# Linear attention on one core: two of four output banks scaled into SBUF, output products issued as two groups around a turning of keys

## The chip, the core and the metric

One NeuronCore of a Trainium2 chip runs the whole program. The metric is the device time of one execution in microseconds; less is better. The core has TensorE (PE; its weight loads are listed as PEld), VectorE (DVE), ScalarE (ACT), GpSimd (POOL) and SyncE (SP), each with its own instruction queue that is worked in order, and 16 DMA engines. SBUF is the working memory, PSUM the memory of eight banks into which TensorE writes.

## What is computed

The input is x, 8 batches of 1024 rows of 256 channels, all in float32. A convolution block is followed by four layers of linear attention, a feed-forward block with GELU, and a second feed-forward block whose weights are composed from 32 of 64 low-rank pieces. The change lies in the attention layers:

```python
def linear_attention(x, Wq, bq, Wk, bk, Wv, bv, g, bb):
    q = gelu(x @ Wq + bq) + 0.21
    k = gelu(x @ Wk + bk) + 0.21
    v = x @ Wv + bv
    q_r, k_r = rope(q), rope(k)
    # 16 heads of 16 channels
    kmean = jnp.mean(k, axis=2, keepdims=True)
    z = 1.0 / (jnp.einsum('bhnd,bhmd->bhnm', q, kmean) + 1e-06)
    kv = jnp.einsum('bhnd,bhne->bhde', k_r, v) / n
    out = jnp.einsum('bhnd,bhde->bhne', q_r, kv) * z
    return layernorm(out + x, g, bb)
```

## The kernel before

The program has three stages. The convolution stage fills the first 150 us or so, the attention stage runs to about 955 us, and then the pieces of the second feed-forward block are composed and the two feed-forward blocks run to the end.

The attention stage works in 32 **units**. A unit n is one layer of one batch (1024 rows); four batches are interleaved, so a unit depends on the unit four places before it. Each engine has a fixed order of work for a unit, written out by hand, and the engines meet through counting semaphores. `Waits.wait_ge` leaves out a wait that an earlier one already covers.

PSUM is held as four banks `big0` to `big3` and a ring of four banks `ring0` to `ring3`. In unit n the `big` banks hold, one after the other, the turned rows (`turn_u`), the outputs of unit n-1 (`outputs`) and the values of unit n (`values`). The ring serves in turn the four projections of keys, the four turnings of keys (`turn_k`), the four projections of queries, the denominators and the key-value sums.

**PE in unit n** (from line 935): `key_value(n-1)`, `turn_u(n, 1)`, four projections of keys of six 512-column products each, `turn_k` 0 and 1, `outputs(n-1)`, `turn_k` 2 and 3, four projections of queries, `values` 0 to 3 of twelve 256-column products each, `turn_u(n+1, 0)`, `denominators(n)`. `outputs` is 32 products on 32x32 corners of the array, each recorded twice, so 64 records (L928); the first half of them belongs to the first block of channels, the second half to the second. `values(n, u)` writes over `big[u]`, so it waits until bank u of unit n-1 has been added to the residual (`s_y`).

**DVE in unit n** (from line 1150): the end of the normalisation of older units, then `rotate_k` 0 (L1076, L1077), `k_mean`, `rotate_k` 1, and the steps of `FINISH` for unit n-1. For each bank i these are `turn` (L1096, a 32x32 block transpose in the bank), `scale` (L1103, times z) and `add_h` (L1109, the bank plus the residual row block `y_of`, which is in SBUF). `rotate_k` 2 and 3 stand between the first of them. Then come `rotate_q` (L1090, L1091, the rotation of the second half of the queries into `qc` and `qs`) and `split_u(n+1, 0)` (L1065). `turn` waits for `s_out`, which the last output product raises.

**POOL in unit n**: `residual` (L789, L792), four `sum_k` (L773), `rotate_q` of the first half of the queries (L799, L800), `sum_q(n)` (L807), `invert`. `sum_q` waits for DVE's `rotate_q` and issues two DMAs that add `qs` into `qc`. `outputs(n)`, one unit later, waits for their landing (`d_qr`). Six times in the stage, POOL also issues the load of a layer's weights (L760), right after `invert`. The operands of L773, L799 and L800 are all in SBUF.

**The end of the stage.** PE runs `key_value(31)`, then `outputs(31)`, and then enters the composing stage through `then(e, lambda: None)`: `compose_phase` calls the function given to it (`last`) after its first `multiply`. That first `multiply` is twelve 512-column products (L32, L33, L34 into `acc`), and it waits for DVE's first two splittings (L1832, L1834).

## Time and profile before

| what | value |
|---|---|
| median of 3 runs | 1804.67 us |
| lowest and highest | 1802.76 and 1806.49 us |
| the profiled execution's own time | 1804.48 us |
| its span, first to last instruction | 1802.5 us |
| mean granted TensorE clock | 0.994 |
| busy PE, PEld, DVE | 1772.3, 1440.9, 1483.2 us |
| busy ACT, POOL | 922.5, 997.3 us |

The span is 2 us less than the time of the same execution. The busy times are sums over stages that differ: POOL is busy 9 tenths and more in the slices from about 160 to 850 us and mostly idle after, DVE is around 9 tenths in the attention stage and PE shows almost no idle time anywhere. A product's recorded duration is longer than its place in the stream, since products overlap in the array: what one costs is the distance from its start to the next start. Times of rows are microseconds from the span's start, durations are microseconds in timelines and nanoseconds in groups.

### The profile page before, as it was taken

How to read it: one execution, taken by the hardware profiler on the slowest of the kernel's cores; microseconds unless marked ns; L12 is line 12 of the kernel's file. 1: busy time of each engine (PE TensorE's matmuls, PEld its weight loads, DVE VectorE, ACT ScalarE, POOL GpSimd, SP SyncE). 2: the span in 40 equal slices, each digit the busy share in tenths (PEclk: the TensorE clock that was granted, in tenths of full speed). 3: DMA queues.
4: the chain of work that ended last, by engine and by line, in shares of the span. 5: the costliest groups of instructions: out<-in, count | busy, mean ns of one | idle time of the engine just before them, and what ended most of it. 6: DMA issues, size and time to landing. Idle time of an engine off the chain costs nothing.

```text
span 1802.5 us, 42043 instructions
## 1 busy us (share of the span) xinstructions
PE 1772.3 (98%) x17084; PEld 1440.9 (80%) x17084; DVE 1483.2 (82%) x3486; ACT 922.5 (51%) x1741; POOL 997.3 (55%) x775
## 2 busy tenths in 40 slices
PE   9999999999999999999998999999999999999998
PEld 3336788888888888888886988888888888888887
DVE  3667799999999999999997749696979788888887
ACT  4555666777766777766776723332333333332231
POOL 1556999999999999999991022121313121212221
PEclk9999999999999999999999999999999999999999
DMA  7363442122325422323238711010101010101000
GB/s 285 148 255 146 135 113 48 39 70 48 84 49 153 137 65 49 83 49 76 70 92 274 241 62 48 24 47 24 47 24 47 24 48 24 36 35 36 30 7 24
DMA packets 30193, 148.59 MB, mean 82 GB/s; under 512 B 5488, under 2 KB 6320, under 8 KB 20784
## 3 DMA queue, kind: packets, MB, share of 16 engines
q1 hardware_dynamic: 20960, 89.62, 14.1%
q0 software_dynamic: 6272, 46.14, 11.5%
q10 hardware_dynamic: 2768, 10.15, 1.5%
q8 instruction: 134, 2.20, 0.5%
q14 instruction: 59, 0.48, 0.1%
HBM read 80.89 MB, written 31.46 MB: 62 GB/s over the span
## 4 chain that ended last, share of the span: by engine, by line
PE 92%; DVE 3%; DMA 2%; POOL 1%; issue 1%; ACT 1%; ACTq 0%; SPq 0%; DVEq 0%; POOLq 0%
PE bankC L1433 13%; PE bankC L33 7%; PE bankC L32 7%; PE bankC L34 7%; PE ring L32 6%; PE ring L34 6%; PE ring L33 6%; PE bankC L1432 6%; PE big L32 3%; PE big L853 3%; PE big L33 3%; PE big L34 3%; PE ring L873 3%; PE hid_ps L245 3%; PE conv_ps L256 3%; PE big L928 2%
## 5 line engine op out<-in xcount | busy, mean ns | idle before, releaser
L1433 PE MATMUL bankC<-down,act_hi 128*128 128x512 f32 x992 | 353.1, 397 | 0.0
L1432 PE MATMUL bankC<-down,act_lo 128*128 128x256 f32 x868 | 246.2, 284 | 0.0
L1433 PEld LDWEIGHTS bankC<-down,act_hi 128*128 128x128 f32 x992 | 186.3, 188 | 41.9
L1558 DVE TENSOR_TENSOR act_lo<-gel,act_hi 128x512 fp32r<-128x512 f32 x256 | 210.6, 823 | 8.7
L33 PE MATMUL bankC<-aT_lo,up_hi 128*128 128x512 f32 x512 | 199.6, 390 | 0.0
L32 PE MATMUL bankC<-aT_hi,up_hi 128*128 128x512 f32 x512 | 199.5, 390 | 0.0
L34 PE MATMUL bankC<-aT_hi,up_lo 128*128 128x512 f32 x512 | 199.4, 389 | 0.0
L1512 POOL TENSOR_TENSOR hC<-hC,vecC 128x1024 f32<-128x1024 f32 x16 | 38.7, 2416 | 283.9 <-PE turn L1407 283.9
L1518 POOL TENSOR_TENSOR rstdC<-var_epsC,minus_halfC 128x4 f32<-128x4 f32 x47 | 56.1, 1194 | 249.2 <-DVE var_epsC L1586 249.2
L1432 PEld LDWEIGHTS bankC<-down,act_lo 128*128 128x128 f32 x868 | 164.1, 189 | 1.4
L773 POOL TENSOR_TENSOR kr<-kr,kc 128x512 f32<-128x512 f32 x128 | 161.8, 1296 | 0.2 <-DVE kr L1077 0.2
L1475 ACT ACTIVATE aT_hi<-turn 128x512 fp32r<-128x512 f32 x64 | 34.8, 596 | 234.8 <-PE turn L1407 234.8
L1483 ACT ACTIVATE gel<-bankC,b1s 128x512 f32<-128x512 f32 x128 | 88.5, 691 | 128.7 <-PE bankC L34 112.6
L792 POOL TENSOR_TENSOR yB<-yB,shift 128x1024 f32<-128x1024 f32 x64 | 152.2, 2408 | 0.0
L1483 ACT ACTIVATE gel<-bankC 128x512 f32<-128x512 f32 x128 | 76.8, 600 | 141.7 <-PE bankC L34 125.0
L1004 ACT ACTIVATE yB<-yB,offset,rstdB 128x256 f32<-128x256 f32 x256 | 129.5, 590 | 0.0
L973 ACT ACTIVATE gkT<-ring,bias_qk 128x512 f32<-128x512 f32 x128 | 88.2, 690 | 79.7 <-PE ring L34 79.7
L1547 DVE TENSOR_TENSOR aT_lo<-turn,aT_hi 128x512 fp32r<-128x512 f32 x64 | 41.1, 683 | 105.2 <-ACT aT_hi L1475 105.2
L1076 DVE SCALAR_TENSOR_TENSOR kc<-ring,cos_k 128x512 f32<-128x512 f32 x128 | 86.6, 677 | 42.7 <-PE ring L873 42.7
L998 ACT ACTIVATE v<-big 128x512 f32<-128x512 f32 x128 | 76.5, 598 | 85.6 <-PE big L34 85.5
L789 POOL TENSOR_TENSOR yB<-yB,gain 128x1024 f32<-128x1024 f32 x48 | 114.5, 2405 | 0.1
L34 PEld LDWEIGHTS bankC<-aT_hi,up_lo 128*128 128x128 f32 x512 | 96.1, 188 | 20.2
(211 smaller groups left out, 5224.0 us busy)
## 6 DMA issues: line engine op xcount, KB each, us to landing
qc<-qs POOLq DMA_DIRECT2D x64, 512.0 KB, 6.5
raw_late<-in_AB SPq DMA_DIRECT2D x30, 320.0 KB, 3.8
u<-hA SPq DMA_DIRECT2D x8, 1024.0 KB, 4.8
u_next<-u SPq DMA_DIRECT2D x8, 1024.0 KB, 5.7
hC<-u SPq DMA_DIRECT2D x16, 512.0 KB, 4.2
xC<-in_x SPq DMA_DIRECT2D x16, 512.0 KB, 5.1
out<-w_flat SPq DMA_DIRECT2D x15, 512.0 KB, 2.6
w_flat<-in_AB SPq DMA_DIRECT2D x22, 320.0 KB, 4.2
```

Source lines behind the costliest of these rows:

```text
L32: e.matmul(out, wh, xh, start=start, stop=False)
L33: e.matmul(out, wh, xl, start=False, stop=False)
L34: return e.matmul(out, wl, xh, start=False, stop=stop)
L773: e.tensor_tensor(kr[:, u, :], kr[:, u, :], kc[:, u, :], ALU.add).then_inc(s_kr, 1)
L789: e.tensor_tensor(tiles(y, a), tiles(src, a), row(gain), ALU.mult).then_inc(s_mul, 1)
L792: e.tensor_tensor(tiles(y, a), tiles(y, a), row(shift), ALU.add).then_inc(s_res, 1)
L973: e.activation(gkT[:, db, half(x)], ring_of(n, "k", 2 * x + db)[:, :], ACT.Gelu, bias=bias_qk[:, at:at + 1], accum_out=k_sums[:, db, x:x + ...
L1004: e.activation(y[:, o, :], y[:, o, :], ACT.Identity, bias=offset[:, two, o:o + 1], scale=rstd[:, two, o:o + 1]).then_inc(s_unit, 1)
L1432: e.matmul(bank[:, 0:H], a_lo[:, fb, tok], both[k][:, fb, 0, :], start=False, stop=False)
L1433: m = e.matmul(bank[:, :], a_hi[:, fb, tok], both[k][:, fb, :, :].rearrange("p a h -> p (a h)"), start=fb == 0, stop=fb == FB - 1)
L1483: e.activation(gel[:, n % GEL, :], bank_of(i, k, s, fb)[:, :], ACT.Gelu if k == 0 else ACT.Gelu_apprx_tanh, bias=b1s[:, fb:fb + 1] if k == ...
L1558: e.tensor_tensor(a_lo[:, fb, :], g, a_hi[:, fb, :].bitcast(F32), ALU.subtract).then_inc(s_act_lo, 1)
```

## The change

Six edits, all in the attention stage:

1. `scale` of banks 2 and 3 writes its result into SBUF, into the second half of `qs` (`apart`), in place of the bank itself; `add_h` of banks 2 and 3 reads it there.
2. `values` 2 and 3 wait for the scaling of their bank (`s_scaled`), no more for the adding.
3. DVE's `rotate_q` gets a wait for those two adds (the same engine, earlier in its order), since it writes where they read.
4. The order of `FINISH`: `turn` 2 before `add_h` 0, and `scale` 3 before `add_h` 2. `rotate_k` 3 now comes before `turn` 1.
5. `outputs(n-1)` is issued as two groups of 16 products, with `turn_k(n, 2)` between them. The semaphore for DVE is raised by the last product of the second group.
6. `outputs(31)` is handed to the composing stage, which runs it after its first `multiply`.

```diff
@@ -690,6 +690,9 @@
+        HELD = 2
+        apart = lambda i: qs[:, i - HELD, half(1)]
@@ -876,7 +879,10 @@
             def values(n, u):
                 wt = weights(n, 2 * H, H)
-                w.wait_ge(s_y, 4 * (n - 1) + u + 1)
+                if u < HELD:
+                    w.wait_ge(s_y, 4 * (n - 1) + u + 1)
+                else:
+                    w.wait_ge(s_scaled, 4 * (n - 1) + u + 1)
                 w.wait_ge(s_lo, 4 * n + 4)
@@ -912,7 +918,7 @@
-            def outputs(n):
+            def outputs(n, blocks=range(CB)):
...
-                for db in range(CB):
+                for db in blocks:
                     for j in range(QUARTERS):
...
-                m.then_inc(s_out, 1)
+                if CB - 1 in blocks:
+                    m.then_inc(s_out, 1)
@@ -940,8 +947,10 @@
                 turn_k(n, 1)
                 if n >= 1:
-                    outputs(n - 1)
+                    outputs(n - 1, [0])
                 turn_k(n, 2)
+                if n >= 1:
+                    outputs(n - 1, [1])
                 turn_k(n, 3)
@@ -952,8 +961,7 @@
             key_value(UNITS - 1)
-            outputs(UNITS - 1)
-            then(e, lambda: None)
+            then(e, lambda: outputs(UNITS - 1))
@@ -1086,6 +1094,7 @@
                 w.wait_ge(s_out, n)
+                w.wait_ge(s_y, 4 * (n - 1) + HELD + db + 1)
                 w.wait_ge(d_q, 2 * 16)
@@ -1098,15 +1107,17 @@
+                to = out if i < HELD else apart(i).rearrange("p (a n d) -> p a n d", a=TILES, d=HD)
...
-                e.tensor_tensor(out, out, zb, ALU.mult).then_inc(s_scaled, 1)
+                e.tensor_tensor(to, out, zb, ALU.mult).then_inc(s_scaled, 1)
 
             def add_h(n, i):
                 heads = y_of(n)[:, :, 64 * i:64 * i + 64]
+                sums = big[i][:, :] if i < HELD else apart(i)
...
-                e.tensor_tensor(heads, big[i][:, :].rearrange("p (a m) -> p a m", a=TILES), heads, ALU.add).then_inc(s_y, 1)
+                e.tensor_tensor(heads, sums.rearrange("p (a m) -> p a m", a=TILES), heads, ALU.add).then_inc(s_y, 1)
@@ -1146,8 +1157,8 @@
-            FINISH = [[(turn, 0)], [(turn, 1), (scale, 0)], [(add_h, 0), (turn, 2)], [(scale, 1), (add_h, 1)],
-                      [(turn, 3), (scale, 2)], [(add_h, 2), (scale, 3)], [(add_h, 3)]]
+            FINISH = [[(turn, 0)], [(turn, 1), (scale, 0)], [(turn, 2), (add_h, 0)], [(scale, 1), (add_h, 1)],
+                      [(turn, 3), (scale, 2)], [(scale, 3), (add_h, 2)], [(add_h, 3)]]
@@ -1170,10 +1181,10 @@
                     rotate_k(n, u)
-                    if n >= 1 and u < 3:
-                        finish(n - 1, u - 1)
+                    if n >= 1 and u == 1:
+                        finish(n - 1, 0)
                 if n >= 1:
-                    for k in range(2, 7):
+                    for k in range(1, 7):
                         finish(n - 1, k)
```

## Rows read from the trace of the kernel before

**Rows 1.** Timeline of DVE, unit 19: start, duration, engine, line, operands [idle before].

```profile
637.01 0.72 DVE L1096 STREAM_TRANSPOSE big<-big 128x512 f32<-128x512 f32 x1
...
644.37 0.67 DVE L1103 TENSOR_TENSOR big<-big,z 128x512 f32<-128x512 f32 x1
645.07 0.69 DVE L1109 TENSOR_TENSOR yB<-big,yB 128x512 f32<-128x512 f32 x1
...
646.41 0.69 DVE L1109 TENSOR_TENSOR yB<-big,yB 128x512 f32<-128x512 f32 x1
647.01 0.68 DVE L1090 SCALAR_TENSOR_TENSOR qc<-ring,cos_q 128x512 f32<-128x512 f32 x1
```

**Rows 2.** Waits by engine, line and releaser, 192 to 1010 us: total, times, longest.

```profile
PEld ring L32 <- DVE kr L1077: 7.7, 29, 0.3
...
PEld big L32 <- DVE yB L1109: 1.8, 12, 0.2
```

**Rows 3.** Timeline of POOL, units 18 to 20.

```profile
625.55 1.78 POOL L807 DMA_DIRECT2D qc<-qs  x2 [1.36 <-DVE qs L1091]
...
643.70 1.30 POOL L799 TENSOR_TENSOR qc<-gT,cos_q 128x512 f32<-128x512 f32 x1
...
650.04 1.78 POOL L807 DMA_DIRECT2D qc<-qs  x2 [1.28 <-DVE qs L1091]
...
668.92 1.29 POOL L799 TENSOR_TENSOR qc<-gT,cos_q 128x512 f32<-128x512 f32 x1
```

**Rows 4.** Line L807, the two DMAs issued at 650.0 and 650.7.

```profile
DMA to landing us min/median/max: 5.2/6.6/7.9
```

**Rows 5.** Timeline of PE, unit 19; the third row is from a cut at 635.25.

```profile
633.90 1.04 PE L873 MATMUL ring<-identity,gkT 128*128 128x128 f32 x8
634.87 1.49 PE L928 MATMUL big<-qc,kv 32*32 32x256 f32 x64
...
634.87 0.71 PE L928 MATMUL big<-qc,kv 32*32 32x256 f32 x32
...
636.30 1.09 PE L873 MATMUL ring<-identity,gkT 128*128 128x128 f32 x8
```

**Rows 6.** Timelines of PE and DVE where outputs waited for their DMA.

```profile
857.73 1.49 PE L928 MATMUL big<-qc,kv 32*32 32x256 f32 x64 [1.71 <-DMA qc<-qs]
...
859.27 0.73 DVE L1096 STREAM_TRANSPOSE big<-big 128x512 f32<-128x512 f32 x1 [1.09 <-PE big L928]
```

**Rows 7.** Line L1558: nanoseconds min/median/max; then one of its long ones, beside POOL's.

```profile
L1558 DVE TENSOR_TENSOR act_lo<-gel,act_hi x256: 691/693/2782, 1061.1 to 1785.0; 128x512 fp32r<-128x512 f32 x128
...
1090.03 2.77 DVE L1558 TENSOR_TENSOR act_lo<-gel,act_hi 128x512 fp32r<-128x512 f32 x1
...
1089.74 2.52 POOL L1523 TENSOR_TENSOR w_flat<-w_flat,xC 128x1024 f32<-128x1024 f32 x1 [4.16 <-DVE w_flat L1598]
```

**Rows 8.** Timelines of DVE and POOL at 158 us.

```profile
158.67 1.76 DVE L600 TENSOR_TENSOR bias_v<-bv_in,head_block 128x256 f32<-128x256 f32 x1
...
157.76 4.92 POOL L789 TENSOR_TENSOR yB<-u_next,gain 128x1024 f32<-128x1024 f32 x2 [1.46 <-PE big L853]
```

**Rows 9.** Timelines of DVE and POOL at 1049 us.

```profile
1049.10 1.35 DVE L1832 SCALAR_TENSOR_TENSOR duo_lo<-w_flat,w_col,duo_hi 128x1024 fp32r<-128x1024 f32 x1 [5.82 <-ACT duo_hi L1801]
1050.38 2.56 DVE L1834 TENSOR_TENSOR duo_lo<-w_flat,duo_hi 128x256 fp32r<-128x256 f32 x1
...
1049.45 3.20 POOL L1514 TENSOR_TENSOR hC<-hC,vecC 128x1024 f32<-128x1024 f32 x1
```

**Rows 10.** Timelines of DVE and PE at the end of the attention stage.

```profile
949.61 1.22 DVE L1834 TENSOR_TENSOR duo_lo<-u_next,duo_hi 128x1024 fp32r<-128x1024 f32 x1
...
954.04 2.38 PE L928 MATMUL big<-qc,kv 32*32 32x256 f32 x64 [5.53 <-DMA qc<-qs]
956.35 0.79 PE L32 MATMUL acc<-duo_hi 128*128 128x512 f32 x1
...
959.82 0.39 PE L32 MATMUL acc<-duo_hi 128*128 128x512 f32 x1
```

## The prediction

> **What bounds the kernel now.** I read the page first (each engine's share and its slices), then a timeline of one attention unit on PE, on DVE and on POOL, then the list of waits, and last the rows in which DVE and POOL touch. The attention units are the part to cost, since all edits but one repeat there. One unit lasts 24.49 us: POOL's DMA issue comes at 625.55 and again at 650.04 [rows 3]. PE is the bound: its only repeated waits over the stage are 0.27 us for a rotated key (29 times) and 0.15 us for an added bank (12 times listed) [rows 2]. DVE and POOL have little room behind it. POOL is idle once a unit, 1.28 us ahead of the DMA issue, because DVE's rotation of queries is not done [rows 3]. And the DMA has less room still: the second of the two is issued at 650.65 and lands 7.9 us after [rows 4], at 658.55, while the outputs that need it start one period after 634.87 [rows 5], at 659.36. So four things run in one ring with small gaps: POOL, DVE, the DMA and PE.
>
> **What the change removes.** The two waits of PE. The third rotation of keys moves ahead of two finishing steps, and values 2 need no add. The two waits are at most 0.27 + 0.15, about 0.4 us a unit [rows 2]; part of it overlaps with products in flight, so I take 0.3. PE alone could then do a unit in about 24.2 us.
>
> **What the split of the outputs adds.** The 64 records start within 1.12 us (1.49 less one duration of 0.37), the first 32 within 0.34 (0.71 less 0.37), and turning starts at 636.30, which is 0.31 after the last start [rows 5]. A group of 32 alone thus takes 0.34 + 0.31 = 0.65, two take 1.30, where the 64 take 1.43: the second half of the 64 is slower than the first, as if the queue ran dry, and the turning between would let it fill. Against that stands one more change between full products and corners: the eight turnings ahead need 0.97 (633.90 to 634.87), at 0.11 each they would need 0.88 [rows 5], so 0.1, and some 0.05 on the way back. Sum: +0.02 us a unit. If the second group runs at the pace of the slow half, it is +0.34; with no cost of changing, -0.13. I take +0.02, because the slow half begins only after 32 records. The rule of the Trainium skill (TensorEngine Tiling (Array Packing), Key Properties) that changing the tiling mode drains the engine speaks against this edit; the trace has its 0.31 us, already in the sum above, and no run here separates the two.
>
> **What moves on DVE.** Turning of the keys comes between the groups, so the semaphore for DVE comes later: 0.65 + four turnings (0.59 with both changes) + 0.34 + 0.37 + 0.05 = 2.0 us after the outputs begin, where it was 1.54 (857.73 to 859.27) [rows 6]. From 634.87 that is 636.87, still ahead of 637.01, when DVE gets there [rows 1]. This delay is hidden as long as the outputs don't start late. The new wait of `rotate_q` for the adds costs nothing: they stand ahead of it in DVE's own queue. Behind each of DVE's adds, though, everything of DVE is queued, and POOL's DMA issue waits for the rotation.
>
> **What the change adds, and what I hold to decide it.** The adds of banks 2 and 3 read two operands from SBUF; before, one was in PSUM. POOL at that time runs products whose operands are both in SBUF, without a gap. The trace shows what two such operations do to each other. L1558 takes 0.69 us, but 2.77 at 1090.03, when POOL's 2.52 us add had begun at 1089.74; it ends 0.54 after POOL's, so it really ran from 0.15 before POOL's end. At 158.67 DVE waits inside the first of two adjoining operations of POOL and ends at 160.43, long before the second ends at 162.68: it gets in between the two [rows 8]. At 1049.45 POOL waits until DVE's first is done, and DVE's second, behind it in the queue, waits until POOL's is done at 1052.65 [rows 9]. They exclude each other and take turns [rows 7 to 9]. The Trainium skill says so too (SBUF — State Buffer, "SBUF: two separate sides": the pair of ports is an exclusive lock against DVE operations with two SBUF inputs), not who goes next; by that rule as by the rows, the sum is the one below, and without the exclusion it is the first rival.
>
> **The ring, step by step.** Count from POOL's DMA issue D.
> - POOL's first product of queries starts at D + 18.15 (625.55 to 643.70) and takes 1.30 [rows 3]. DVE can get in at D + 18.15 + 1.30 - 0.15 = D + 19.30.
> - DVE asks for its first SBUF add 8.57 us after the first turn: 8.06 as before (637.01 to 645.07), plus 0.6 for the scaling that now precedes it, less 0.1, since add 2 no longer stands right behind its own scaling (0.70 against 0.60 us) [rows 1].
> - Add 2 runs at D + 19.30. POOL then takes its turn: held until add 2 is nearly done, 0.69 - 0.2, then 1.30, less 0.15. Add 3 starts about 1.66 after add 2.
> - The rotation starts 0.60 after that, and the next D is 3.03 later (647.01 to 650.04) [rows 1, 3].
>
> Sum: 19.30 + 1.66 + 0.60 + 3.03 = 24.59 us a unit, against 24.49. So PE's gain of 0.3 isn't had: PE is early, and waits at the outputs. The DMA's way round agrees: it lands at D + 8.5 (7.9 plus 0.61 between the issues), outputs, 2.0 to the first turn, 8.57 to the request, D + 19.13 with 0.05 for the wake-up, only 0.17 ahead of D + 19.30.
>
> **The sum.** 29 units at +0.10: +2.9. Six units have the weight load on POOL, where the first product comes at 18.88 (650.04 to 668.92) [rows 3]; in a ring without room its 0.73 counts: +4.4. The first two units, in which the ring has to settle: two delays of POOL of 0.4 each, twice, an estimate: +1.5. The unit in which the DMA waits anyway (1.71 us) [rows 6] loses about 1 more, since the DMA is issued later; small hiccups of PE elsewhere, an estimate of the same size, are now covered by its waits: together 0. Sum of the units: +8.8.
>
> The end of the stage: the DMA lands at 954.04, the outputs and the first twelve composing products are done at 959.82, 5.8 us later [rows 10]. After the change the twelve run while the DMA is under way: their operand is ready at 949.61 + 1.22 = 950.83, they need 2.7 at full rate (0.227 each). Behind the landing stay the outputs, 1.5 to 2.3. That saves 3.5 to 4.3; the first products behind an idle PE are slow (0.79 for the first at 956.35 against 0.39), which may push them past the landing, and I take 3.2, from 1.5 to 4.3. Nothing behind it changes: the composing stage is PE's.
>
> Total: +8.8 - 3.2 = +5.6 on the profiled execution, 1804.48 + 5.6 = 1810.1; that execution lies 0.2 under the median of the runs, so 1810.
>
> **The rivals.**
> - *The exclusion is small or DVE gets both adds at once.* Then the ring needs at most 19.30 + 0.6 + 0.6 + 3.03 = 23.5, PE is the bound at 24.2, 29 units save 8 us and the end 4: 1793 (1790 to 1800). Against it: [rows 7, 9]. For it: no row shows two adjoining DVE adds beside short POOL products. 0.25.
> - *The request comes too late.* If the outputs' split costs 0.17 more, or the DMA lands 0.17 later, DVE asks after D + 19.30 and waits for the next product, 1.25 more a unit. In all units that is +36: 1846; in half of them about 1828. This is where the split decides, though its own time is nothing. 0.2.
> - *POOL's queue always wins.* DVE then waits for the end of all four products (18.15 + 5.0) and a unit is about 27.4: +85, 1890. [rows 8] speak against it. 0.05.
> - *No change*, since the gains and exclusions meet: 1805. 0.05.
>
> The forecast itself, 1803 to 1816, has 0.45.
>
> **How the numbers follow.** A measurement tells about 0.2%, 3.6 us. The forecast's own range lies two thirds above +3.6. Slower: 0.32 of the forecast, 0.2 and 0.05: 0.57. Same: 0.1 + 0.05 + 0.03 = 0.18. Faster: 0.03 + 0.22 = 0.25. The range leaves out the last tenth of the first rival and the worst of the late ones: 1792 to 1836.
>
> **What would show it.** L1109 in two groups, one near 0.69 and one over a microsecond long; POOL's L799 or L800 lengthened by about 0.4; a period of 24.6; a PE wait of 0.3 to 0.5 for the DMA ahead of L928 in most units. If L1109 stays at 0.69 throughout, the first rival holds. Periods near 25.8 are the second. If PE waits for neither the rotated key nor an added bank, the removed waits are right, whatever the time. At the end, L928 stands behind twelve products into acc.

## The result and the profile after

| what | before | after |
|---|---|---|
| median of 6 runs, us | 1804.85 | 1846.67 |
| lowest and highest, us | 1802.76, 1808.12 | 1840.18, 1852.39 |
| span of the profiled execution, us | 1802.5 | 1844.4 |
| mean granted TensorE clock | 0.994 | 0.988 |
| busy DVE, POOL, us | 1483.2, 997.3 | 1563.3, 1013.8 |

The ratio is 1.0227, with a 95% interval of 1.0203 to 1.0252: slower by 41 us. The forecast was 1810 with a range of 1792 to 1836. The direction was right, the time lies outside the range.

**The adds.** The line of the adds (L1109 of before is L1120 here), nanoseconds min/median/max, first the banks read in PSUM, then those read in SBUF:

```profile
L1120 DVE TENSOR_TENSOR yB<-big,yB x64: 659/680/693, 197.8 to 1021.2; 128x512 f32<-128x512 f32 x64
L1120 DVE TENSOR_TENSOR yB<-qs,yB x64: 669/1777/6000, 201.6 to 1029.2; 128x512 f32<-128x512 f32 x64
```

DVE is busy 80 us more than before, and the second row accounts for that and a little more: the page of the profile has it as 131.8 us for 64, mean 2097 ns, where 64 at the first row's 0.68 would be 44.

**A unit that went as forecast.** Timelines of DVE and POOL of the kernel after, unit 19; columns as in [rows 1, 3]. The DMA issue before it came at 647.35.

```profile
665.78 1.57 DVE L1120 TENSOR_TENSOR yB<-qs,yB 128x512 f32<-128x512 f32 x1
...
665.49 1.32 POOL L802 TENSOR_TENSOR qc<-gT,cos_q 128x512 f32<-128x512 f32 x1
666.74 1.77 POOL L803 TENSOR_TENSOR qs<-gT,sin_q 128x512 f32<-128x512 f32 x1
668.47 1.73 POOL L802 TENSOR_TENSOR qc<-gT,cos_q 128x512 f32<-128x512 f32 x1
...
672.01 1.77 POOL L810 DMA_DIRECT2D qc<-qs  x2 [0.56 <-DVE qs L1100]
```

Add 2 is asked for 0.29 into POOL's first product and ends at 667.35, so it really began at 666.66: 19.31 after the DMA issue, where the forecast had 19.30. POOL's second product carries the delay (1.77 for 1.28). The unit lasts 672.01 - 647.35 = 24.66; forecast 24.59.

**A unit that did not.** The same two timelines, unit 20:

```profile
690.46 5.99 DVE L1120 TENSOR_TENSOR yB<-qs,yB 128x512 f32<-128x512 f32 x1
...
690.88 1.29 POOL L802 TENSOR_TENSOR qc<-gT,cos_q 128x512 f32<-128x512 f32 x1
692.13 1.28 POOL L803 TENSOR_TENSOR qs<-gT,sin_q 128x512 f32<-128x512 f32 x1
693.38 1.26 POOL L802 TENSOR_TENSOR qc<-gT,cos_q 128x512 f32<-128x512 f32 x1
694.61 1.28 POOL L803 TENSOR_TENSOR qs<-gT,sin_q 128x512 f32<-128x512 f32 x1
700.00 1.75 POOL L810 DMA_DIRECT2D qc<-qs  x2 [4.11 <-DVE qs L1100]
```

DVE asks at 690.46, during POOL's last sum of keys, and is served only when POOL's last product is over: four operations of POOL begin and end meanwhile, none of them lengthened. Behind the add stands the rotation of queries, for which POOL then waits idle, 4.11 us. The unit lasts 27.99. I call such an add **passed over** (it lasts over 2.2 us). In the kernel after these are the adds of units 4, 6, 8, 12, 16, 20, 22, 24, 25, 30 and 31: eleven, among them all six in which POOL issues a weight load. The mark of 2.2 us misses the mildest case: unit 28 asks during POOL's third product, sees the fourth go first and lasts 2.10, so by what happens there are twelve.

**Where the 41 us are.** From the DMA issue of unit 2 to that of unit 31 before took 713.13 and after takes 757.95: +44.8. The 713.13 are 24.59 a unit on the average, the forecast's own period: the 24.49 of the forecast is an ordinary unit of the kernel before, and a few of its units last longer, up to 25.8. So the division counts over 24.59 (25.3 with a weight load). Eleven units passed over, at 28.0 or 27.3, cost 2.7 each: 29.5. Four units right behind such a one (7, 17, 21, 23) last 25.9, since DVE asks at the end of POOL's first product or later: 5.2. Unit 13, of the same kind, 27.1: 2.5. Unit 28, 27.2: 2.6. The six weight loads, at the forecast's 0.73 each (the served ones in e15 last 25.2): 4.4. The twelve other units, 24.57 to 24.69: 0.6. Sum 44.8. Before unit 2 the kernel gains 0.9, and from the DMA issue of unit 31 to the end it gains 2.1. 44.8 - 0.9 - 2.1 = 41.8, and the spans differ by 41.9.

**Why the next unit is late too.** Behind a passed-over add PE stands idle for 2.1 to 3.2 us ahead of its projections of keys. The table by windows has us, then busy time of PE, PEld, DVE, ACT and POOL with counts, then the granted TensorE clock, the DMA share and GB/s; first the window behind the add of unit 6, then that behind the add of unit 4:

```profile
338.16:341.16 3.00, 3.00 (x9) 2.31 (x9) 2.96 (x10) 0.78 (x2) 2.92 (x4) 0.54 1.00 199
286.25:289.25 3.00, 2.84 (x13) 2.02 (x13) 2.96 (x10) 1.47 (x4) 2.92 (x4) 1.00 0.97 194
```

Of ten such places, five have a granted clock of 0.50 to 0.65 there, most of the time its lower level of 1.2 GHz, and they are just the five ahead of units 7, 13, 17, 21 and 23. The keys' 512-column products then start 0.43 apart and not 0.23, the outputs begin 8.7 to 10.0 after the DMA issue and not 7.7, and DVE asks 0.9 to 2.2 later. In the other five the clock stays at 1.00 and the next unit isn't late. Why it fell in some and not in others the rows don't tell; the idle times before are alike. (Ahead of unit 21 the DMA lands 8.4 after its issue, where 7.0 to 7.9 is usual, and would have made that unit late by itself.) In unit 28 it is the DMA alone: it lands 10.1 after its issue, and PE waits 2.36 for it.

**What was removed is gone.** Waits by engine, line and releaser over the attention stage, 192 to 1030 us; neither row of [rows 2] has an answer here. What PE waits for now is of another kind:

```profile
PEld ring L32 <- issue: 41.2, 33, 3.4
...
PE ring L32 <- DVE hT_lo L1073: 30.2, 24, 3.2
```

PE stands ahead of the projections of keys, because DVE's splitting of the input stands behind the adds in DVE's queue. The forecast had PE wait at the outputs for the DMA in most units; in the same list that wait comes 11 times and to 5.6 us in all (PEld, L934).

**The outputs in two groups.** PE's timeline of unit 19, answering [rows 5], and DVE's first turn:

```profile
655.09 0.71 PE L934 MATMUL big<-qc,kv 32*32 32x256 f32 x32
655.73 0.66 PE L876 MATMUL ring<-identity,gkT 128*128 128x128 f32 x4
656.32 0.71 PE L934 MATMUL big<-qc,kv 32*32 32x256 f32 x32
...
656.96 0.44 PE L876 MATMUL ring<-identity,gkT 128*128 128x128 f32 x2
...
657.22 0.73 DVE L1105 STREAM_TRANSPOSE big<-big 128x512 f32<-128x512 f32 x1
```

0.64 + 0.59 + 0.64, as forecast (0.65, 0.59, 0.65). The first turn starts 2.13 after the outputs; forecast 2.0, before 1.54.

### The profile page after: what moved, and what is told of

The parts are those of the page before. It is cut to its first block, busy times and chain, and to the rows that moved or that the text cites. A ratio compares the mean times of both kernels' runs of the same rounds, so it can differ in the third digit from the quotient of the medians.

```text
span 1844.4 us, 42105 instructions
## 1 busy us (share of the span) xinstructions
PE 1783.0 (97%) x17084; PEld 1437.6 (78%) x17084; DVE 1563.3 (85%) x3486; ACT 922.7 (50%) x1741; POOL 1013.8 (55%) x775
## 4 chain that ended last, share of the span: by engine, by line
PE 69%; DVE 22%; issue 5%; DMA 3%; POOL 1%; ACT 1%; ACTq 0%; SPq 0%; DVEq 0%; POOLq 0%
PE bankC L1444 13%; PE bankC L32 7%; PE bankC L33 7%; PE bankC L34 7%; DVE yB L1120 6%; PE bankC L1443 6%; PE ring L32 4%; PE ring L33 3%; PE ring L34 3%; DVE kr L1085 3%; PE conv_ps L256 3%; PE hid_ps L245 3%; DVE big L1105 2%; DMA qc<-qs 2%; DVE hT_lo L1073 2%
## 5 line engine op out<-in xcount | busy, mean ns | idle before, releaser
L1444 PEld LDWEIGHTS bankC<-down,act_hi 128*128 128x128 f32 x992 | 186.3, 188 | 41.9
L795 POOL TENSOR_TENSOR yB<-yB,shift 128x1024 f32<-128x1024 f32 x64 | 152.6, 2416 | 0.0
L1120 DVE TENSOR_TENSOR yB<-qs,yB 128x512 f32<-128x512 f32 x64 | 131.8, 2097 | 0.0
L1558 DVE TENSOR_TENSOR aT_lo<-turn,aT_hi 128x512 fp32r<-128x512 f32 x64 | 41.1, 684 | 105.2 <-ACT aT_hi L1486 105.2
L32 PE MATMUL ring<-hT_hi,w_second 128*128 128x512 f32 x256 | 106.8, 417 | 17.7 <-DVE hT_lo L1073 17.4
L32 PE MATMUL ring<-hT_hi,w_first 128*128 128x512 f32 x256 | 104.5, 408 | 14.0 <-DVE hT_lo L1073 13.7
```

The lines of the kernel that those rows point to most:

```text
L32: e.matmul(out, wh, xh, start=start, stop=False)
L795: e.tensor_tensor(tiles(y, a), tiles(y, a), row(shift), ALU.add).then_inc(s_res, 1)
L1120: e.tensor_tensor(heads, sums.rearrange("p (a m) -> p a m", a=TILES), heads, ALU.add).then_inc(s_y, 1)
L1444: m = e.matmul(bank[:, :], a_hi[:, fb, tok], both[k][:, fb, :, :].rearrange("p a h -> p (a h)"), start=fb == 0, stop=fb == FB - 1)
```

## The experiments

No kernel leaves out part of the computation. Ratios are to the kernel before on the same chip, with 95% intervals; e13, e14 and e16 to e19 rest on two executions each, the others on four or more. Counts and periods are from one profiled execution of each kernel. "Units passed over" counts adds of bank 2 over 2.2 us in units 3 to 31: six with a weight load, 23 others. The diffs are against the kernel after, where nothing else is said.

### First question: is it the SBUF adds, the split, the order or the end?

**e1_psum_adds**: all four banks scaled in place and added from PSUM; order, split and end as in the kernel after.

```diff
-        HELD = 2
+        HELD = 4
...
-                w.wait_ge(s_y, 4 * (n - 1) + HELD + db + 1)
```

> The changed kernel with banks 2 and 3 scaled in place in PSUM again and added from there, values waiting for the adds; the new order of the finishing steps, the two groups of outputs and the moved last outputs stay. If the exclusion between DVE's adds with two SBUF operands and POOL's products makes the loss, the add takes 0.69 us in every unit, a unit takes 24.2 to 24.4 us and the time is 1793 (1789 to 1799). If the split of the outputs or the new order makes it, the time stays at 1835 to 1850.

Measured: 1815.14, ratio 1.0050 (1.0033 to 1.0067). No add lasts over 0.7. So 32 of the 41 us at the least belong to the two SBUF operands. But the unit lasts 24.95, not 24.2 to 24.4, so this kernel pays some 13 us that the kernel after doesn't, and the operands' share is larger (e3 gives 51). The waits of this kernel show why: values wait for an added bank once in nearly every unit, at most 0.7. The two rows are the weight load and the product behind it in the same wait.

```profile
PEld big L32 <- DVE yB L1119: 22.3, 30, 0.7
PE big L32 <- DVE yB L1119: 16.2, 30, 0.5
```

In the new order the add of bank 2 stands behind the scaling of bank 3, and a rotation of keys stands ahead of both. That order needs the early release of the bank which the scaling into SBUF gives; alone it costs 0.46 a unit. I had not expected it.

**e6_psum_one_group**: the same with the outputs in one group.

```diff
-                    outputs(n - 1, [0])
-                turn_k(n, 2)
-                if n >= 1:
-                    outputs(n - 1, [1])
+                    outputs(n - 1)
+                turn_k(n, 2)
```

> The kernel after with all four banks scaled in place and added from PSUM, and the outputs in one group: beside the first run (the same with two groups, 1815.1, period 24.95) it takes the split away. If the order of scaling and adding (values 2 waiting 0.7 us for their bank) is the whole of its +0.46 a unit, this one stays at 1813 to 1816. If the split with its later first turn is what makes the adds late, the wait of values 2 shrinks by up to 0.5 and the time falls to 1803 to 1806.

Measured: 1812.73, ratio 1.0040 (1.0027 to 1.0054), period 24.95 again. The order is the cost, not the split.

**e2_one_group**: the kernel after with that same edit.

> The changed kernel with the 32 output products in one group ahead of the third turning, everything else kept. If the exclusion alone makes the loss, the ring from one DMA issue to the next stays at 24.65 us in the units where DVE gets in after one product, units with an add of 5 to 6 us stay too, and the time is 1830 to 1855. If the split makes DVE ask too late for a place between two products, the time falls to 1815 or less and the adds of 5 us are gone.

Measured: 1842.91, ratio 1.0204 (1.0184 to 1.0224), an interval that overlaps that of the kernel after. Served units last 24.6, and eleven are passed over (4, 5, 8, 10, 12, 13, 16, 18, 20, 24, 26). The split is not the cause.

**e9_split_only**: the kernel before with the outputs in two groups and nothing else (the edit of e6, the other way round).

> The kernel before with the outputs in two groups around the third turning, nothing else. By the prediction's sum the PE stream grows by 0.02 us a unit (-0.13 to +0.34) and DVE's first turn comes 0.5 later after the start of the outputs, hidden if DVE arrives later anyway: 1805 to 1806. The rival, that the later turn reaches DVE, POOL's DMA issue and back to PE: up to +0.5 a unit, 1820. In the trace the period of a unit (24.49 before) tells: 24.50 by the first, up to 25.0 by the rival.

Measured: 1805.35, ratio 1.0004 (0.9995 to 1.0013), period 24.5. The split costs nothing that can be measured, and gains nothing.

**e5_end_only**: the kernel before with the end's edit.

```diff
-            outputs(UNITS - 1)
-            then(e, lambda: None)
+            then(e, lambda: outputs(UNITS - 1))
```

> The kernel before with the edit of the end alone (outputs of unit 31 behind the first twelve composing products). The sum of the prediction says -3.2 us (1.5 to 4.3), so 1801.3; the kernel after lost 2.05 between D(31) and the end, and if that is this edit's worth, 1802.4. The rival that the products behind the landing are no quicker in sum says 1804.5. In the trace: L928 of unit 31 behind twelve products into acc, end of L928 to end of span shorter by 2 to 3.

Measured: 1801.06, ratio 0.9982 (0.9973 to 0.9991), so -3.2 (-4.9 to -1.6). Its PE timeline, answering [rows 10]:

```profile
954.26 0.47 PE L34 MATMUL acc<-duo_hi,duo_lo 128*128 128x512 f32 x1
954.66 1.49 PE L928 MATMUL big<-qc,kv 32*32 32x256 f32 x64
956.09 0.50 PE L32 MATMUL acc<-duo_hi 128*128 128x512 f32 x1
```

Twelve products and the outputs are done at 956.1, before at 959.8. In the kernel after only 2.1 is gained between the DMA issue of unit 31 and the end. There PE had been idle for 6.67, and its first nine products ran at 1.2 GHz, as the table by windows shows. That isn't where the rest was lost, though: all twelve are over before the DMA lands, and the outputs wait for it.

```profile
993.00:997.00 4.00, 3.78 (x9) 3.05 (x10) 4.00 (x8) 0.00 (x0) 3.12 (x2) 0.50 0.92 175
...
993.22 0.77 PE L32 MATMUL acc<-duo_hi 128*128 128x512 f32 x1 [6.67 <-DVE duo_lo L1845]
...
998.79 1.49 PE L934 MATMUL big<-qc,kv 32*32 32x256 f32 x64 [0.74 <-DMA qc<-qs]
```

From the DMA issue of unit 31 to the thirteenth composing product it is 13.6 in the kernel before, 10.3 in e5 and 10.1 in the kernel after: up to there the edit gives 3.4 and 3.6. The kernel after loses 1.4 of it again somewhere behind; where, wasn't followed. In e7, where unit 31 is served, 2.4 is gained from that DMA issue to the end.

### Second question: can the adds be taken out of POOL's way?

**e3_adds_after_rotation**: banks 2 and 3 are held in another buffer (the second half of `gkT`, free until the next projections of keys), and both adds stand behind the rotation of queries. POOL's products are then over when DVE asks, or the last of them is running, and nothing of the ring waits for the adds. ScalarE, which writes the next keys there, waits for the adds.

```diff
-        apart = lambda i: qs[:, i - HELD, half(1)]
+        apart = lambda n, i: (gkT if n + 1 < UNITS else qs)[:, i - HELD, half(1)]
...
                 for db in range(CB):
                     rotate_q(n, db)
+                if n >= 1:
+                    finish(n - 1, 6)
```

> The changed kernel with the scaled banks 2 and 3 kept in the second half of gkT (idle by then) and both adds moved behind the rotation of queries, where POOL issues its DMAs and has no product with two SBUF operands. If the exclusion makes the loss, the adds take 0.69 us, POOL's DMA issue comes 1.2 us earlier in the ring, and the time is 1792 (1788 to 1798), under the kernel before. If an add from SBUF is slow for itself, or DMA issue excludes DVE as well, the adds stay over 1 us and the time is 1815 or more.

Measured: 1795.9, ratio 0.9951 (0.9932 to 0.9970). It beats both kernels. The DVE timeline of unit 19; POOL's next DMA issue is at 668.85:

```profile
665.79 0.68 DVE L1100 SCALAR_TENSOR_TENSOR qc<-ring,cos_q 128x512 f32<-128x512 f32 x1
...
668.18 1.52 DVE L1121 TENSOR_TENSOR yB<-gkT,yB 128x512 f32<-128x512 f32 x2
...
668.85 1.75 POOL L810 DMA_DIRECT2D qc<-qs  x2 [0.30 <-POOL qs L803]
```

The two adds take 1.52 together; in unit 19 of the kernel after they took 3.27. POOL now waits for its own last product and not for DVE; the period is 24.15, which agrees with the 24.2 I gave PE alone. Against the kernel after this is 51 us less with the same computation: the price of the adds standing where POOL's chain and the ring are.

**e10_after_rotation_one_group**: e3 with the outputs in one group.

> The version with its two SBUF adds behind the rotation of queries (1795.9, ratio 0.995, period 24.15), with the outputs in one group again. There PE bounds the unit, so the split shows by its own cost: the prediction's +0.02 a unit says 1795 to 1796 (ratio 0.995); if two groups are quicker as the groups alone were (0.65 twice for 1.43, so -0.13), this one is slower, up to 1800; if the later turn costs, it is quicker, 1790 or less.

Measured: 1797.38, ratio 0.9956 (0.9941 to 0.9972), period 24.15. With and without the split the times can't be told apart, where PE is the bound too.

### Third question: why is DVE passed over in some units and not in others?

**e4_breath**: a memset of one column (0.09 us) on POOL ahead of each of its four products. Extra work.

```diff
+                e.memset(breath[:, 2 * db:2 * db + 1], 0.0)
                 e.tensor_tensor(qc[:, db, cols], gT[:, db, cols], table_q(cos_q, db, x), ALU.mult)
+                e.memset(breath[:, 2 * db + 1:2 * db + 2], 0.0)
                 e.tensor_tensor(qs[:, db, cols], gT[:, db, cols], table_q(sin_q, db, x), ALU.mult).then_inc(s_qr, 1)
```

> The changed kernel with a one-column memset on POOL ahead of each of its four products of queries, so that no product follows directly on another. If DVE's add is passed over because POOL's next product is already in line, there is no add over 2.2 us left, all units take 24.7 to 25.9 us, and the time is 1810 to 1825. If being passed over has another cause, adds of 5 to 6 us stay in some 10 units and the time is 1840 or more.

Measured: 1838.4, ratio 1.0182 (1.0165 to 1.0199). Passed over: 0 of 23 ordinary units, but 6 of 6 with a weight load. Neither theory foretold that split. It says that there are two cases, and that the load units are one by themselves. (Unit 2, which the count leaves out, was passed over with the memsets in place, 3.6 us.)

**e7_again**: the kernel after once more.

> The kernel after once more, unchanged, to see which units are passed over in another execution. If a fixed property of the program decides, the same eleven (4, 6, 8, 12, 16, 20, 22, 24, 25, 30, 31) are passed over and the span is 1844 within 1. If the phase of the moment decides, the six with the load stay and the others change, by number too, with 3 us for each unit more or less: 1840 to 1852.

Measured: 1847.08, ratio 1.0224 (1.0206 to 1.0243). The six with the load are passed over again, and of the others 3, 13, 14, 17, 18 and 21, where the first execution had 6, 22, 25, 30 and 31. The load units are fixed, the rest is not.

**e11_load_later** and **e12_pool_later**: the load moves the products 0.7 later. Is it this place that loses, or the load?

```diff
-                if lane(n) == 0 and 2 <= n // LANES + 1 < B // LANES * L:
-                    load_w(n // LANES + 1)
...
                     rotate_q(n, 0, db)
+                if lane(n) == 0 and 2 <= n // LANES + 1 < B // LANES * L:
+                    load_w(n // LANES + 1)
                 sum_q(n)
```

> The kernel after with POOL's six weight loads behind the products of queries instead of ahead of the residual. In three kernels all six units with the load had their add of bank 2 passed over (5.8 to 6.1 us), 18 of 18, and in all of them it was asked for during the last sum of keys, since the load put POOL's products 0.7 later. Theory one, the place in POOL's chain decides: the six become like the others (mostly served after the first product, 24.65), which gives back about 6 x 3.4 = 20: 1826, 1818 to 1836, and at most two or three of the six are passed over. Theory two, the load itself or chance decides: the six stay near 28, 1840 to 1850.

Measured: 1853.69, ratio 1.0249 (1.0218 to 1.0281): no quicker than the kernel after, whose interval overlaps, and above both expectations. Passed over: 1 of 6 load units and 5 of 23 others, so the load's place matters. But the time was lost again at once: the queries' DMA now queues behind the weight load. Line L810 has

```profile
DMA to landing us min/median/max: 4.5/6.7/13.1
```

where the longest in the kernel after is 9.5. PE waits for it at the outputs in five units, here in unit 5:

```profile
294.51 1.17 PE L934 MATMUL big<-qc,kv 32*32 32x256 f32 x32 [5.33 <-DMA qc<-qs]
```

```diff
                     load_w(n // LANES + 1)
+                elif n >= 3:
+                    w.wait_ge(s_memset, 1)
+                    for s in range(2):
+                        e.tensor_tensor(spare[:, s:s + 1], tiny[:, :], minus_half[:, 0:1], ALU.pow)
                 residual(n)
```

> The kernel after with about 0.7 us of extra work on POOL (two powers of one column) at the head of every unit that has no weight load, so that in all units the add is asked for during the last sum of keys. Extra work, nothing left out. Theory one, the place decides: nearly all units from the fourth on are passed over, period about 28, time 1804.7 + 29 x 3.5 = about 1905 (1890 to 1915), which is the third rival of the prediction. Theory two, the place doesn't decide: the share of units passed over stays at a third and the others run at 25.3, time 1860 to 1875.

Measured: 1870.39, ratio 1.0351 (1.0334 to 1.0368). Passed over: 6 of 6 and 9 of 23. Of the ordinary units whose request fell into a sum of keys, eleven were served and three passed over. The place does not decide; theory one fell, and the load itself was left.

**e14_load_after_residual** puts the load behind the residual, right ahead of the sums of keys. **e13_small_load** puts a small DMA at the load's place in all other units from unit 3 on.

```diff
-                if lane(n) == 0 and 2 <= n // LANES + 1 < B // LANES * L:
-                    load_w(n // LANES + 1)
                 residual(n)
+                if lane(n) == 0 and 2 <= n // LANES + 1 < B // LANES * L:
+                    load_w(n // LANES + 1)
```

> The kernel after with the weight load issued between POOL's residual and its sums of keys, 10 us later than in the kernel after, so that its transfer (9 us) is in flight while the add is asked for. If the load as such decides wherever it stands ahead of the sums, all six units stay passed over (28.0): 1840 to 1852. If only its place ahead of the residual does, they become like the others: 1825 to 1840.

Measured: 1851.3, ratio 1.0257 (1.0227 to 1.0287); 6 of 6 and 8 of 23.

```diff
                     load_w(n // LANES + 1)
+                elif n >= 3:
+                    w.wait_ge(d_spare, 16 * small[0])
+                    small[0] += 1
+                    e.dma_start(spare[:, :], w_split[0:1, :, 0:2].rearrange("l p c -> (l p) c")).then_inc(d_spare, 16)
                 residual(n)
```

> The kernel after with a small DMA (two columns) issued by POOL at the head of every unit from the fourth on that has no weight load, at the load's place. Extra work, nothing left out. Seen so far: with the load ahead of the chain the add was passed over in 30 of 30 units (five kernels), with 0.7 us of arithmetic in its place (the run with POOL later) in about 9 of 23, and with the load behind the products in 1 of 6. If an issued DMA ahead of the residual is what keeps DVE out until the chain ends, nearly all units are passed over now: period about 28, 1895 to 1915. If it is the load's own bulk or chance, about a third as before: 1855 to 1880.

Measured: 1900.24, ratio 1.0528 (1.0490 to 1.0566). Passed over: 6 of 6 and 22 of 23, period 27.9 to 28.0 throughout (the one missing, unit 28, lasts 2.0 and was passed by one product). A DMA of two columns, issued by POOL 14.7 us ahead of DVE's request, is enough. From the timelines of POOL and DVE, unit 17:

```profile
628.57 0.63 POOL L830 DMA_DIRECT2D spare<-w_split  x1
...
643.27 5.93 DVE L1126 TENSOR_TENSOR yB<-qs,yB 128x512 f32<-128x512 f32 x1
```

**e15_load_before_invert** and **e16_invert_first**. The queries' two DMAs stand ahead of POOL's chain in every unit, though, and do no such harm. Between them and the chain lies `invert`: a power (L818), then a product that waits for that power (L820). e15 puts the load ahead of `invert`, e16 takes `invert` from between the queries' DMAs and the chain.

```diff
                 sum_q(n)
+                if lane(n + 1) == 0 and 2 <= (n + 1) // LANES + 1 < B // LANES * L:
+                    load_w((n + 1) // LANES + 1)
                 if n >= 2:
                     invert(n - 2)
```

> The kernel after with the weight load moved two POOL instructions earlier, behind the two DMAs of queries and ahead of the power (L818) and product of invert, so that it delays no DMA of queries. Small DMAs ahead of the residual made 28 of 28 adds be passed over, but the DMAs of queries, which stand ahead of the power, don't. Theory one: a DMA issued with no power behind it is what keeps DVE out; then the six units are served like the others (at most three passed over) and the time falls by about 18: 1820 to 1835. Theory two: any load DMA ahead of the chain does it: all six passed over, 1840 to 1855.

Measured: 1824.85, ratio 1.0107 (1.0077 to 1.0137). Passed over: 0 of 6 and 4 of 23. Two POOL instructions' difference in place gives back 22 us. Rows of POOL and DVE, unit 16, which has a load:

```profile
561.06 1.21 POOL L763 DMA_DIRECT2D w_second<-w_split  x1
561.65 2.31 POOL L818 TENSOR_TENSOR rstdB<-var_epsB,minus_halfB 128x8 f32<-128x8 f32 x1
564.04 0.20 POOL L820 TENSOR_TENSOR offset<-minus_mean,rstdB 128x8 f32<-128x8 f32 x1
...
578.71 1.75 DVE L1120 TENSOR_TENSOR yB<-qs,yB 128x512 f32<-128x512 f32 x1
```

```diff
-                sum_q(n)
                 if n >= 2:
                     invert(n - 2)
+                sum_q(n)
```

> The kernel after with POOL's invert ahead of its DMAs of queries, so that in every unit a DMA stands directly ahead of the residual and the chain. The chain then starts 2.5 us earlier after the DMA issue (15.7), the request falls into the third product, and being passed over costs little: add 2 ends at D + 20.5 and not 19.3. Theory one: nearly all units are passed over (add 2 takes about 2.7 us, only 0.68 for add 3), period 24.8, with the load 25.4: 1811 to 1820. Theory two: about a third are, and the others show add 2 at about 1.5 and add 3 at 1.78: 1806 to 1815. The count of long adds tells them apart, not the time.

Measured: 1831.63, ratio 1.0138 (1.0118 to 1.0159). Passed over: 6 of 6 and 21 of 23. The count is what theory one said; the time was 12 over its range, since the period is 25.3 (25.9 with the load) and not 24.8. POOL's and DVE's rows of unit 18:

```profile
634.49 1.83 POOL L802 TENSOR_TENSOR qc<-gT,cos_q 128x512 f32<-128x512 f32 x1
635.75 1.82 POOL L803 TENSOR_TENSOR qs<-gT,sin_q 128x512 f32<-128x512 f32 x1
637.00 2.62 POOL L818 TENSOR_TENSOR rstdB<-var_epsB,minus_halfB 128x8 f32<-128x8 f32 x1
...
634.80 3.32 DVE L1120 TENSOR_TENSOR yB<-qs,yB 128x512 f32<-128x512 f32 x1
```

The products start 1.26 apart and are recorded as lasting 1.83: here each overlaps the next by 0.57, where in the kernel after it is 0.03. The two units that weren't passed over say more. In units 28 and 29 POOL stood idle between the DMAs and the chain, 1.66 for DVE and 0.55 for PE. There the records overlap by 0.04 to 0.05 again, and the add of unit 29 got in (that of 28 asked during the last product). POOL's rows of unit 29:

```profile
900.10 4.76 POOL L792 TENSOR_TENSOR yB<-yB,gain 128x1024 f32<-128x1024 f32 x2 [0.55 <-PE big L856]
...
914.50 1.30 POOL L802 TENSOR_TENSOR qc<-gT,cos_q 128x512 f32<-128x512 f32 x1
```


**e17_small_load_power**, **e18_small_load_product** and **e19_small_load_own_wait** take e13 and put parts of `invert` behind the DMA. All have extra work.

```diff
+                if n >= 3:
+                    w.wait_ge(s_memset, 1)
+                    e.tensor_tensor(other[:, :], tiny[:, :], minus_half[:, 0:1], ALU.pow)
                 residual(n)
```

> The kernel with the small DMA in every unit (1900 us, 29 of 29 adds passed over from unit 3 on but 28), with a power of one column behind that DMA, also behind the weight load, and no wait of POOL for itself. Extra work, nothing left out. Theory one, a power behind the DMA undoes its effect: the count falls to a third or less (0 to 12 of 29), period of the others about 25.8: 1845 to 1875. Theory two, it was the wait of invert for its own result or its second instruction that did it: the count stays at 28 or 29, 1905 to 1920.

Measured: 1917.01, ratio 1.0623 (1.0590 to 1.0656); 6 of 6 and 23 of 23. With `mult` in place of `pow`:

> The same with an ordinary product of one column in the power's place. If any instruction of another size or kind behind the DMA undoes the effect, the count falls as with the power. If only the power does, the count stays at 28 or 29 of 29 and the time at 1900 to 1912; the residual behind the DMA is ordinary arithmetic too and doesn't undo it, so this is what I expect.

Measured: 1906.18, ratio 1.0563 (1.0530 to 1.0596); 6 of 6 and 22 of 23. Neither undoes the DMA's effect.

```diff
+                if n >= 3:
+                    w.wait_ge(s_memset, 1)
+                    e.tensor_tensor(other[:, 0:1], tiny[:, :], minus_half[:, 0:1], ALU.pow).then_inc(s_own, 1)
+                    own[0] += 1
+                    w.wait_ge(s_own, own[0])
+                    e.tensor_tensor(other[:, 1:2], other[:, 0:1], tiny[:, :], ALU.mult)
                 residual(n)
```

> The kernel with the small DMA and the one-column power (29 of 29 adds passed over), and behind them a one-column product that waits, by a semaphore, for that power's result, as invert's second instruction does. Extra work, nothing left out. Theory one, a wait of POOL for its own result behind the DMA undoes the effect: the count falls to a third or less, 1850 to 1885. Theory two, it was the length of invert's power (2.28 us against 0.59 for one column) or something else: the count stays at 28 or 29, 1918 to 1930.

Measured: 1861.29, ratio 1.0318 (1.0266 to 1.0371); 1 of 6 and 5 of 23. POOL's and DVE's rows of one unit:

```profile
663.62 0.63 POOL L832 DMA_DIRECT2D spare<-w_split  x1
664.27 0.59 POOL L835 TENSOR_TENSOR other<-tiny,minus_halfB 128x1 f32<-128x1 f32 x1
664.93 0.19 POOL L838 TENSOR_TENSOR other<-other,tiny 128x1 f32<-128x1 f32 x1
...
678.28 1.79 DVE L1134 TENSOR_TENSOR yB<-qs,yB 128x512 f32<-128x512 f32 x1
```

With more work on POOL than e17 this kernel is 56 us quicker. So the power, the wait for its result and the product together undo the DMA's effect, and a power or a product alone doesn't. A second short instruction without the wait was not tried.

A wait for its own result isn't enough by itself, though. The residual has two, in every unit: each of its adds (L795) waits by semaphore for the product two places ahead (L792). In the kernel after they stand behind the weight load of unit 20, whose add was passed over:

```profile
675.78 0.64 POOL L763 DMA_DIRECT2D w_first<-w_split  x1
676.44 4.76 POOL L792 TENSOR_TENSOR yB<-yB,gain 128x1024 f32<-128x1024 f32 x2
681.15 4.76 POOL L795 TENSOR_TENSOR yB<-yB,shift 128x1024 f32<-128x1024 f32 x2
```

The results are there in time and POOL doesn't stop. In `invert` and in e19 the result is that of the instruction right ahead, and POOL stands idle for 0.08. That sorts the units better than the wait does. The thirteen profiles with these adds in POOL's chain have 377 units from 3 to 31. In 150 of them POOL is nowhere idle by over 0.03 between its last DMA and DVE's request, and all 150 are passed over. In the other 227 it is idle at least once; 169 are served, 50 passed over, and 8 asked during the last product. (Here an add counts as passed over if a product that began after its request went first, so three of 2.0 to 2.1 us are in.)

### The counts side by side

| kernel | what stands between POOL's last DMA and its chain | load units passed over | other units |
|---|---|---|---|
| after; again; e2 | load units: nothing; others: `invert` | 6, 6, 6 of 6 | 5, 6, 5 of 23 |
| e4 (memsets between products) | as after | 6 of 6 | 0 of 23 |
| e12 (two powers, no DMA) | load units: nothing; others: `invert` and the powers | 6 of 6 | 9 of 23 |
| e14 | load units: nothing, not even the residual | 6 of 6 | 8 of 23 |
| e11, e15 | `invert` in all units | 1, 0 of 6 | 5, 4 of 23 |
| e13, e16 | nothing in all units | 6, 6 of 6 | 22, 21 of 23 |
| e17, e18 | one power, one product | 6, 6 of 6 | 23, 22 of 23 |
| e19 | a power and a product that waits for it | 1 of 6 | 5 of 23 |

"Nothing" means nothing at which POOL stood idle (but for units 28 and 29 of e16); the residual's operations, with their two waits, lie there in all but the load units of e14. Unit 2 is outside the counts: it has a DMA and no `invert` ahead of its chain, and its add was passed over in seven of the thirteen profiles and got in in six. So the rule of 150 in 150 is one of units 3 to 31, not of every place.

## Why the prediction was wrong

**Right.** The two waits of PE are gone. The period of a served unit was forecast at 24.59 and is 24.6 to 24.7, by the same steps (19.30 against 19.31 to the start of add 2). The exclusion between DVE's two-SBUF add and POOL's products is real. The split costs nothing that can be measured (e9: +0.7, -0.9 to +2.3; forecast +0.02 a unit, 0.6 in all). The end is worth 3.2 (e5), as forecast; in the kernel after 2.1 of it is left. PE alone at 24.2: e3 runs at 24.15.

**The step that failed** is the sentence "They exclude each other and take turns". The exclusion had three groups of rows, [rows 7 to 9]; that DVE gets in between two operations of POOL rested on one event, [rows 8], in another stage, with two long operations of POOL. It was read as a rule, and the third rival, that POOL's queue wins, was set at 0.05 on its strength and only for all units together. In the kernel after it wins in 11 of 29 units, at the price which that rival had worked out (27.4; measured 27.3, with a load 28.0). The case "in some of the units" stood nowhere, and it is the one that happened: 29.5 of the 41 us, and with the late units behind them 37. That the measured 1846.7 is the second rival's 1846 is chance: only six units ask too late, and eleven have the third's cause.

**The second rival** was right in kind, as a follower: in five units behind a passed-over one DVE asks too late for the place after POOL's first product (four last 25.9, unit 13 lasts 27.1), 7.7 us together. Its 1.25 a unit was measured as 1.3. But the cause was neither the split nor the DMA, as I had it: it was TensorE's granted clock of 0.50 to 0.65 behind PE's idle stretch. Unit 28 alone is late by its DMA.

**The way round by the DMA** was reckoned wrong without harm. By [rows 4] the request was to come at D + 19.13, 0.17 ahead of the place. In the kernel after the outputs start 7.75 after the DMA issue in an ordinary unit, without a wait for the DMA, and DVE asks at D + 18.44 (unit 19: 18.43), 0.86 ahead. The 8.57 from the first turn to the request held (8.56), and the DMA took less: 7.0 to 7.9 from its issue, where the sum had 8.5.

**The ordinary units.** The sum took +0.10 for each of 29 over an ordinary unit of 24.49. The kernel before takes 24.59 on the average of these units, so a served unit at 24.64 costs 0.05.

**The weight load** was priced for the 0.73 it takes on POOL, +4.4. Its real price was the state in which it leaves POOL's chain: e15, where it stands two instructions earlier, is 22 us quicker. A moved or added DMA on POOL was weighed by its time alone.

**The first two units** were put at +1.5 and came out at -0.9, in e7 at +2.15: unit 2 is passed over there. **The end** came out at 2.1 in place of 3.2, though the edit gave its 3.6 up to the thirteenth composing product; what lost the rest stays open.

**A rule and the rows.** The 1.57 of a served add and the 5.99 of one passed over are both DVE waiting for POOL. The Trainium skill (SBUF — State Buffer, "SBUF: two separate sides") says that whichever starts first has the pair of ports for its whole instruction and the other blocks. The served units agree; in the passed-over ones DVE stays blocked over up to five instructions of POOL (unit 20), four of which begin after its request, so by the measurement what has waited longer doesn't always go first.

**What stays open.** Two things. First, why an idle moment of POOL behind a DMA frees its chain, and whether the idle moment or the wait does it. In e19 they come together; unit 29 of e16, idle for PE's sake, is the only one that parts them. POOL's records in e16 overlap by 0.57, as if its parts ran out of step, so that the next product holds the ports before the last one is through, and after the idle moment by 0.04 to 0.05. The Trainium skill (Perfetto Trace Analysis, "DMA Instruction — SWDGE (GPSIMD)") says that the descriptors of such a DMA are generated by two of that engine's processors, which would put them behind the others. Against this stands that in e13, where DVE is passed over as surely, the overlap is 0.03. This is an argument, not shown. Second, why about a quarter of the ordinary units are passed over (24 of 92 in after, again, e2 and e14), and different ones in each execution. The phase of the request does not sort them: in the kernel after unit 25 asked 0.27 into POOL's first product and was passed over, unit 26 asked 0.27 into it and was served after it. In e4 the memsets removed this case in units 3 to 31 (0 of 23).

## What to carry to other kernels

A DVE operation with both inputs in SBUF beside a chain of POOL operations should be priced twice: once for getting in after one operation, once for waiting until the whole chain is over, with a share of units for each; and it should be placed where nothing waits for it, as e3 does. Two waits of 0.3 us were removed here at the price of putting an uncertain 1 to 5 us into the one ring without room. When one instruction decides a ring, a single row from another stage shows what can happen, not what will, and a range that allows "in some of the units" is the honest one.

## What the runs showed of the hardware

- DVE's add with two SBUF inputs lasts 0.68 alone. In the kernel after add 2 lasts 0.7 to 1.9 when it gets in after the product in flight, by how late it asks, and 4.9 to 6.0 in the eleven units where it is passed over. Beside POOL's power (L818 in e16) and its DMA issue (e3) the same add lasts 0.67 to 0.68.
- After a DMA issued by POOL, its later operations on SBUF kept DVE out to the end of their chain (e13, e16, e17, e18: 112 of 116 units by the mark of 2.2 us), unless POOL had been idle once in between (e15, e19: 10 of 58). A DMA of two columns does it as well as one of a layer's weights. In unit 2 it did so in seven of thirteen profiles only.
- A DMA queued behind a weight load on POOL's queue landed after up to 13.1 us (e11), where 9.5 was the longest in the kernel after.
- Behind ten stretches of 2.1 to 3.2 us in which PE was idle, TensorE's granted clock stayed at 1.00 in five and was 0.50 to 0.65 in the other five (kernel after).
